# Identity transposes between the products of the first 12 expert tiles, and a multiplication moved from VectorE to GpSimd

## The reference, cut to what matters

```
h_sh = gelu(x @ Wfc_sh);  shared_out = h_sh @ Wproj_sh          # every token, 2 experts
combine = softmax of the two best scores of a token              # 8 experts, 2 taken
h_r = gelu(x @ Wfc_r);    routed_out = sum combine * (h_r @ Wproj_r)
out = x + shared_out + routed_out
```

## Time and profile before

| | |
|---|---|
| time, median of 3 runs (lowest to highest) | 1442.15 us (1441.43 to 1442.72) |
| the profiled execution: its time, its span | 1444.6 us, 1442.8 us |
| busy share of the span: PE, DVE, ACT, POOL | 81%, 57%, 45%, 42% |
| mean granted TensorE clock | 0.907 |
| tile loop of f0, first transpose to last y copy | 288.2 to 522.2 us |
| tile loop of f1, first transpose to last y copy | 1138.8 to 1393.4 us |

### The profile page before, as it was taken

How to read it: one execution, slowest core, us unless ns; L and a number is a source line. 1 busy time by engine, 2 the same in 40 slices (tenths; PEclk the granted TensorE clock), 3 DMA queues, 4 the chain that set the end, 5 groups by cost and what they waited for, 6 DMA issues and landing times. The chain is left out here.

```text
span 1442.8 us, 31655 instructions
## 1 busy us (share of the span) xinstructions
PE 1175.6 (81%) x11702; PEld 988.7 (69%) x11702; DVE 829.6 (57%) x1805; ACT 649.3 (45%) x1171; POOL 600.1 (42%) x622
## 2 busy tenths in 40 slices
PE   6979989919996889689999999968997718886840
PEld 4766666819996867468888888856767718885840
DVE  6859978403221324358888888847986615553541
ACT  5327754304453424155666656536772103452410
POOL 4742323264444235544343433333342463444255
PEclk9999998959997999899999999999997959997975
DMA  6002215012221121100000000001105011221122
GB/s 171 9 2 66 51 24 202 14 46 49 57 65 47 46 85 32 44 6 1 0 0 0 0 0 0 1 6 19 21 9 196 25 45 43 60 58 46 42 79 69
DMA packets 61906, 62.62 MB, mean 43 GB/s; under 512 B 12592, under 2 KB 50864, under 8 KB 61296
## 3 DMA queue, kind: packets, MB, share of 16 engines
q1 hardware_dynamic: 51824, 42.52, 9.9%
q0 software_dynamic: 9088, 18.63, 5.2%
q10 hardware_dynamic: 896, 0.17, 0.1%
HBM read 42.67 MB, written 16.52 MB: 41 GB/s over the span
## 5 line engine op out<-in xcount | busy, mean ns | idle before, releaser
L1963 PE MATMUL f_bank<-f_xT,f_w_tile 128*128 128x128 f32 x1248 | 184.5, 295 | 82.7 <-issue 48.1
L1963 PEld LDWEIGHTS f_bank<-f_xT,f_w_tile 128*128 128x128 f32 x1248 | 167.7, 208 | 88.9 <-issue 50.8
L1975 PE MATMUL f_bank<-f_w_down,f_hidden 128*128 x1248 | 179.2, 290 | 50.8 <-ACT f_hidden L1880 30.0
L1975 PEld LDWEIGHTS f_bank<-f_w_down,f_hidden 128*128 128x128 f32 x1248 | 162.6, 203 | 56.4 <-issue 56.2
L1616 POOL DMA_INDIRECT f_xn<-f_xn_rows,f_source x156 | 148.6, 952 | 47.4 <-issue 47.4
L1424 POOL TENSOR_TENSOR f_turn_cell<-ident 128x1 f32<-128x1 f32 x60 | 12.8, 213 | 319.5 <-issue 107.1
L1627 POOL DMA_INDIRECT f_hot_row<-f_slots_y,f_slots x128 | 122.6, 958 | 39.9 <-issue 39.9
L1050 POOL TENSOR_TENSOR ret_rstd<-ret_var,ret_minus_half 128x8 f32<-128x8 f32 x32 | 52.7, 1647 | 173.5 <-DVE ret_var L1089 173.5
L1880 ACT ACTIVATE f_hidden<-f_before_gelu 128x512 f32<-128x512 f32 x78 | 49.0, 629 | 162.0 <-DVE f_before_gelu L1802 146.4
L1880 ACT ACTIVATE f_hidden<-f_bank 128x512 f32<-128x512 f32 x78 | 46.5, 596 | 149.5 <-remote 83.9
L1868 ACT ACTIVATE f_w_tile<-f_w_up 128x512 f32 x156 | 96.2, 619 | 29.0 <-DVE f_owner L1768 28.2
(11 more groups left out here) (283 smaller groups left out, 2827.8 us busy)
## 6 DMA issues: line engine op xcount, KB each, us to landing
f_slots_y<-f_y_out SPq DMA_DIRECT2D x76, 128.0 KB
a_v_rows<-in_ctx SPq DMA_DIRECT2D x16, 256.0 KB, 4.0
f_xn_rows<-f_xn SPq DMA_DIRECT2D x16, 256.0 KB
f_w_up<-in_f_up SPq DMA_DIRECT2D x1, 2560.0 KB, 10.1
f_w_down<-in_f_down SPq DMA_DIRECT2D x1, 2560.0 KB, 17.1
f_xn<-f_xn_rows,f_source POOLq DMA_INDIRECT x156
X<-in_x SPq DMA_DIRECT2D x4, 512.0 KB, 5.3
kv_ctxT<-in_ctxT SPq DMA_DIRECT2D x8, 256.0 KB, 5.7
```

What stands on the lines that cost most here:

```text
L1963: last = pe.matmul(bank_h[m % 2][:, j * P:(j + 1) * P], w_tile[m % W_RING][:, j * P:(j + 1) * P], xT[m % 2][:], start=True, stop=True)
L1975: last = pe.matmul(bank_y[m % 2][:, 0:D].unsqueeze(1), hidden[m % 2][:, j, :], w_down[:, bass.ds(expert + E0, 1), j, :], start=(j == 0), s ...
```

## The change

Four things change.

1. In the tile loop of both stages, at steps 0 to 11 (`FILLED = 12`), PE issues 3 transposes of the identity (`FILLER = 3`) after the transpose of the tile, and 3 after the up products. They go into bank 7 and signal nobody.
2. In f0 alone, at step 0, PE also issues 24 of them into bank 5 and then waits for `y_added` to reach 3, since bank 7 is one of the two from which DVE adds the shared experts' results.
3. In f1 alone, for the five groups of the first part, POOL multiplies the token numbers in, and DVE doesn't. POOL waits for DVE's `hot_tile` (`hot_tile_set`), and PE's `collect` waits for POOL (`hot_tile_ready`). Everywhere else DVE's own wait before its multiplication is written in another way.
4. The steps at which results are added stand in the stage's specification: in f0 they stay at (63, 69, 75); in f1 they are now (58, 63, 68, 73), so four groups are added inside the loop.

```diff
+    BY_POOL, ADDED_AT = range(first_group[1]) if spec["last"] else (), spec["added_at"]
...
+                for q in BY_POOL:
+                    pool.wait_ge(S["hot_tile_set"], q + 1)
+                    at, N = slice(GTILES * q, GTILES * (q + 1)), counts[0]
+                    shape, out = [P, TOP_K, GTILES, N], hot_tile[q % 2][:, :, :, 0:N]
+                    pool.tensor_tensor(out, out, token_rows[:, at].unsqueeze(1).unsqueeze(3).to_broadcast(shape),
+                                       ALU.mult).then_inc(S["hot_tile_ready"], 1)
...
+                    if q not in BY_POOL:
+                        dve.wait_ge(S["hot_tile_set"], q + 1)
+                        dve.tensor_tensor(out, out, token_rows[:, at].unsqueeze(1).unsqueeze(3).to_broadcast(shape),
+                                          ALU.mult)
...
-                def warm(count):
+                def warm(count, into=bank[7]):
                     for _ in range(count):
-                        pe.transpose(bank[7][:, 0:P], g.ident[:], g.ident[:])
+                        pe.transpose(into[:, 0:P], g.ident[:], g.ident[:])
...
                     pe.wait_ge(S["hot_ready"], q + 1)
+                    if q in BY_POOL:
+                        pe.wait_ge(S["hot_tile_ready"], q + 1)
...
+                    if s == 0 and shared:
+                        warm(8 * FILLER, bank[5])
+                        pe.wait_ge(shared.y_added, FIRST_UNITS // 2)
+                    if s < FILLED:
+                        warm(FILLER)
                     m = s - 1
                     if 0 <= m < M:
                         pe.wait_ge(S["xT_ready"], m + 1)
...
                         last.then_inc(S["up_done"], 1)
+                    if s < FILLED:
+                        warm(FILLER)
...
-ADDED_AT = (63, 69, 75)
+FILLED, FILLER = 12, 3
...
+    ffn_phase(g, "f0", dict(kind="sigmoid", plus_xn=True, part_tiles=(20, 12), last=False, shared=2, following=weights, added_at=(63, 69, 75), gelu=ACT.Gelu, gate_w="f0_gate_w",
...
+    ffn_phase(g, "f1", dict(kind="softmax", plus_xn=False, part_tiles=(20, 12), last=True, shared=0, following=None, added_at=(58, 63, 68, 73), gelu=ACT.Gelu_apprx_tanh,
```

More of the change, by code:

```diff
@@ L1513, in ffn_phase @@
                  "exp_out", "both_ready", "counts_in_psum", "constants_set", "rows_stored", "xn_added",
-                 "owner_ready", "hot_ready", "hot_used", "source_ready", "xT_in_psum", "xT_ready",
+                 "owner_ready", "hot_ready", "hot_tile_set", "hot_tile_ready", "hot_used", "source_ready", "xT_in_psum", "xT_ready",
                  "w_ready", "up_done", "biased", "hidden_ready", "y_in_psum", "y_ready")
@@ L1736, in hot @@
                     shape, out = [P, TOP_K, GTILES, N], hot_tile[b][:, :, :, 0:N]
[L1737 to L1740, removed]
+                    dve.tensor_tensor(out, tile_numbers[:, 0:N].unsqueeze(1).unsqueeze(1).to_broadcast(shape),
+                                      tile_of[:, :, at].unsqueeze(3).to_broadcast(shape), ALU.is_equal)\
+                        .then_inc(S["hot_tile_set"], 1)
+                    if q not in BY_POOL:
+                        dve.wait_ge(S["hot_tile_set"], q + 1)
+                        dve.tensor_tensor(out, out, token_rows[:, at].unsqueeze(1).unsqueeze(3).to_broadcast(shape),
+                                          ALU.mult)
                     shape = [P, TOP_K, GTILES, P]
@@ L1985 @@
 HOT_LATER = (4, 10, 16)
-ADDED_AT = (63, 69, 75)
+FILLED, FILLER = 12, 3
 WARM_START, WARM_COUNT, WARM_BETWEEN, WARM_UP = 28, 88, 6, 24
 def ffn0(g, weights):
-    ffn_phase(g, "f0", dict(kind="sigmoid", plus_xn=True, part_tiles=(20, 12), last=False, shared=2, following=weights, gelu=ACT.Gelu, gate_w="f0_gate_w",
+    ffn_phase(g, "f0", dict(kind="sigmoid", plus_xn=True, part_tiles=(20, 12), last=False, shared=2, following=weights, added_at=(63, 69, 75), gelu=ACT.Gelu, gate_w="f0_gate_w",
                             gate_b="L0_ffn_routing_bias", w_up="f0_up", w_down="f0_down", b_up=None))
 def ffn1(g):
-    ffn_phase(g, "f1", dict(kind="softmax", plus_xn=False, part_tiles=(20, 12), last=True, shared=0, following=None, gelu=ACT.Gelu_apprx_tanh,
+    ffn_phase(g, "f1", dict(kind="softmax", plus_xn=False, part_tiles=(20, 12), last=True, shared=0, following=None, added_at=(58, 63, 68, 73), gelu=ACT.Gelu_apprx_tanh,
                             gate_w="L1_ffn_Wg", gate_b="L1_ffn_bg", w_up="f1_up", w_down="f1_down",
```

## The result

The changed kernel takes 1455.07 us (median of 4 runs, 1452.53 to 1457.03) against 1442.43 for the kernel before (4 runs): a ratio of 1.0084, 95% interval 1.0064 to 1.0104, so 9 to 15 us slower. The profiled execution has a span of 1452.9 us where that of before had 1442.8.

The account below looks back on a forecast made before the run. PE was taken to bound the tile loops after a stall in which POOL's 32 fetches make PE's signals late. The terms 2.6 + 4.8 + 3.8 + 0 + 1.8 = 13.0 on 1442.15 gave 1455 us, range 1436 to 1470.

Parts of the forecast that it names:

- A: Start of f0's loop: tile 1's signal comes only with the held ones, delaying the first down products; +2.6 us, bounds 0 to 4.
- B: Steps 3 to 11 of f0: six transposes a step cost PE 6.2 us, less two waits; +4.8 us.
- The wait of 0.95: A wait in f0's steps 5 to 11, expected to take up one step's 0.69 us of transposes.
- C: Steps 0 to 11 of f1: transposes from step 5 on cost PE 4.5 us, less 0.69 in a wait; +3.8 us.
- D: POOL's multiplication in f1: hidden beside `hot_row`, or +0.45 us to the first group behind it; counted 0, within 0.5.
- E: One more group added inside f1's loop: a 9 us burst moves group 5's first fetch by +1.8 us, bounds -1 to +4.
- one for one: What delays PE's loop delays the last stored result, the fetches and the end by the same amount.
- the clock: Rival: lateness depends on PE's clock, transposes keep it up and more tiles pass in the stall; 1436 us, chance 0.27.
- The hidden transposes: Rival: waits over the rest of the loop take up the transposes; about +1.8 us remains, 1443.9 us, chance 0.11.
- The queue that grows: Rival: each transpose adds lateness, one more group of eight is held per stage, 11.5 us each; 1478 us, chance 0.11.

Follow-up runs that it names:

- mult_alone: The changed kernel, but DVE waits for POOL's multiplication before it makes `hot_row`, so the two don't overlap; 1459.73 us in its one run.
- late_fill: The changed kernel without the transposes at f0's steps 0 to 2 (nor the 24 and their wait) and f1's steps 0 to 5; 1451.29 us, ratio 1.0057 to the kernel before.
- fill_f0: The changed kernel with only f0's identity transposes kept, the 24 and their wait included; f1 as before the change; 1455.23 us, ratio 1.0069 to the kernel before.
- wide_fill: The changed kernel with each three identity transposes replaced by one product of 512 columns; 1466.19 us, ratio 1.0131 to the kernel before.
- fill_f1: The changed kernel with only f1's identity transposes kept; f0, multiplication and order of additions as before the change; 1450.41 us, ratio 1.0041 to the kernel before.
- run 12: Part of "letting POOL run 12 tiles ahead": the kernel before with room for 12 fetched tiles and not 32; 1416.55 us, ratio 0.9810.

## Why the prediction was right, and where only its sum was

The measured 1455.07 is the forecast 1455, but terms of opposite error make up part of that.

- **A** (2.6): 4.1 by the trace (the first down products at 46.0 after the first fetch before, 50.1 after; 3.3 in mult_alone's trace), up to 3.5 by late_fill. The mechanism is the one given: tile 1's signal comes with what was held. Wrong was that the up products of tile 0 are "not later": they are held as well (316.13, one by one, 7.9 later after the first fetch), since the transposes of step 1 stand ahead of them and are let through one at a time too.
- **B** (4.8): 3.6 from tile 3 to tile 12. Every step pays the 0.65 to 0.69, except where a wait or the low clock took it up: tile 3's step, which ran in part at half clock before (2.86 us) and at full clock behind the transposes (2.55), and the waits of 0.70 and 0.40. The wait of 0.95, counted as cover, was none: it grew by 0.31. And a wait that the prediction left out, 0.40 at 349.03, did cover.
- **C** (3.8): 3.5, by another split. Steps 0 to 5 were to cost 0.35 and cost 2.1, since the stall isn't free cover: each transpose takes one of the instructions that PE gets through. Steps 6 to 11 were to cost 3.5 and cost 1.4, since tile 10's step, 3.8 us with its waits, became 2.6, and tile 11's stayed at 4.4: waits of 0.19 and 0.51, which the prediction left out, were cover as well.
- **D** (0, within 0.5): +0.2 to the first `collect` (2.32 us after `hot_tile` began, now 2.50), and as much to f1's first fetch. The overlap was taken for granted in one bound and the block in the other; it is the block, but with a shorter instruction than the 1.0 estimated.
- **E** (1.8): 0.7. The extra burst put the loop's last result 11.3 later (257.0 to 268.3 after the first fetch); less 3.5 for C that is 7.8, where 9.0 was taken from one burst. The 2.79 to the first fetch held (2.82).

By the tile marks A and B together are 7.3 (tile 3 is 3.7 late, tile 12 another 3.6), and A to E 7.3 + 3.5 + 0.2 + 0.7 = 11.7, against 12.6 between the two medians. That the total is hit to a microsecond is luck: A is over its term by more than 1, B and E are each about 1 under, and the runs leave 9 to 15 open. The trace gives part of f0's back behind tile 52 (7.3 to 5.3), fill_f0 doesn't; the prediction's "one for one" is right only within about 2 us.

Of the rivals, the clock falls: no tile more passes in the stall (f0: two by 40 us where there were three), and its clock is as low. In wide_fill the clock of the row is higher, 0.79 and 0.76, and still no tile more passes than before. The hidden transposes fall with fill_f0 and fill_f1. The queue that grows is right in the stall (tile 5 of f1 12.6 late) and wrong about the end, for nearly all of it is given back when the row of fetches ends.

## What to carry to other kernels

Work that is put into an engine's waits is free only if what ends the waits doesn't depend on how much the engine does; here PE got through about 100 instructions in the row of fetches, and idle ones took the place of useful ones. Price such filler at the steps behind the stall, where the engine is the bound, and ask of a long stall first what shortens it: letting POOL run 12 tiles ahead and not 32 gave 27 us (with one run of five that took 3930 us, not explained), where filling it lost 12 or 13.

## What the runs showed that was not expected

- While POOL issues 32 fetches in a row, PE runs 95 to 108 instructions in 40.8 us when there is enough to start; with the change it is some 84 in the first 15 us and then one in about 1.3 us, and instructions without any wait or signal are held too. A signal of products that ended at 9.7 us reaches DVE at 28.5 to 32.8; with 12 fetches in a row it does at 17.4.
- With 12 one-column instructions a step between 16 of 128 columns and a transpose, the granted clock, at 0.50 since the stall, stays there for 50 us in which PE's rows show no gap; with transposes of the identity in their place it is 1.00 (340 to 352).
- A POOL multiplication of 128x376 takes 0.81 us alone and 1.73 beside DVE's `hot_row`.
